# Attention with a low-rank feed-forward layer: one tensor for both q rings, one copy for q's high half, and another order in the DMA queue

## The chip, the cores and the metric

The kernel runs on one core of a Trainium2 chip. The metric is the time of one execution on the device in microseconds. The kernel before takes 2845.18 us, the median of three runs (2844.33 to 2846.65).

## The reference

The input is a batch of 16 sequences of 512 rows with 256 columns. Each row is normalised (layernorm), then goes through causal attention with 32 query heads that share 16 key and value heads in pairs, head width 64, with an ALiBi bias per head, and is added back. The sum is normalised again and goes through a feed-forward layer whose two matrices are products of rank 64, with a gelu between them.

```python
qkv = inputs @ W_qkv                       # 256 -> 2048 (q) + 1024 (k) + 1024 (v)
k, v = repeat(k, 2), repeat(v, 2)          # 16 pairs of query heads
scores = einsum('bhqd,bhkd->bhqk', q, k) / sqrt(64) + slope[h] * (pos_k - pos_q)
scores = where(causal, scores, -inf)
x = x + softmax(scores) @ v @ W_out
P = layernorm(x) @ U1
H = gelu(P @ V1 + b1)
x = x + (H @ U2) @ V2 + b2
```

## The kernel before

Every product is made of fp16 halves: a value is split into a high half and a low half (what is left), and three products (low by high, high by low, high by high) stand for one of fp32. The high half of a projection is made by ScalarE, the low half by VectorE, both out of the PSUM bank into which TensorE projected.

The work is a pipeline over steps. A pass handles one sequence in 16 steps, s = 0 to 15, one step for each key head with its two query heads, and each step has five segments, n = 0 to 4. The first pass fills the pipeline (mode FIRST), 15 passes run full (MID), two more drain it (LAST, TAIL). Within step s these things of different heads lie side by side:

- q of head s is projected (segment 1 of even steps, 2 of odd ones), and in odd steps k of heads s-1 and s together (segment 0).
- `max_scores` (line 509) multiplies q and k of head s-2 for the row maxima, which VectorE takes out of PSUM. After four heads the maxima are transposed (segment 2 of steps 2, 6, 10, 14), split by ScalarE and VectorE (semaphore `lo_m`), and a DMA writes them as two rows (`neg_max_t_hi`, `neg_max_t_lo`) under q, so that the second product of scores already has the maximum taken off. PE waits for these rows at segment 0 of steps 3, 7, 11 and 15.
- `scores` and ScalarE's exponential work on head s-7; ScalarE makes `p_hi`, GpSimd makes `p_lo`.
- `attend` multiplies by v for head s-8, VectorE normalises, ScalarE and GpSimd split the result into the two halves of `o_hi_lo` (GpSimd's half, semaphore `lo_o`, is made in the first segment of the step after), and a transposing DMA brings it into the ring `o_t`. After four heads PE projects them (`project_out`, line 571) and waits for the transposes at segment 4 of steps 12, 0, 4 and 8.
- The feed-forward layer of the sequence before is spread over the remaining places; its result is stored to memory at step 5, and the next sequence's x is loaded at step 1.

q and k are projected two heads to a tile of 128 partitions, but the products of scores want one head with its halves stacked: `q_hi_lo` holds the high half on partitions 0 to 63 and the low half on 64 to 127; `q_hi_aug` holds the high half again, with the ALiBi rows and the maxima's rows below; `k_lo_hi` and `k_hi_aug` are the same for k. So each step copies q by DMA (per step four copies of the high half, two query heads into two rings, and two of the low half), and each odd step k. All these copies, the transposes, the loads and the stores go through one queue, that of SyncE (SP), which issues them in program order: if one waits for a semaphore, all behind it wait. What a step issues, in which order, is written out by hand in `body` of the sync block (from line 379).

TensorE's projections share three PSUM banks. `projection_order` (line 113) lists the uses of a pass in program order, and `PROJ` (line 145) gives use number k the bank k modulo 3; `next_proj` (line 480) makes PE wait until the bank's last user was read. A pass has 76 uses, so the last use of a pass (`out` of step 15, number 75) and the first of the next (`q` of step 0) have the same bank, 0.

Of the kernel before, what the change touches and what calls it, by code (L numbers as in the profile page):

```python
# [23 lines left out]
F16 = mybir.dt.float16  # L24
# [4 lines left out]
P = 128  # L29
D = 256  # L30
DC = D // P
S = 512
# [28 lines left out]
QK_DMAS = 6  # L61
# [50 lines left out]

def projection_order():

    uses = []
    for s in range(KV):
        for n in range(SEG):
            if (s, n) in H_PAIRS:
                uses += [("h", 2 * H_PAIRS[s, n]), ("h", 2 * H_PAIRS[s, n] + 1)]
            if n == MAX_SEG and s % 4 == 2:  # L120
                uses.append(("max", s))
            if (s, n) in X_PAIRS:
                uses.append(("x", X_PAIRS[s, n]))
            if n == K_SEG and s % 2 == 1:
                uses.append(("k", s))
            if n == OUT_SEG:
                uses.append(("out", s))
            if (s, n) in LN2_T_AT:
                uses.append(("ln2", LN2_T_AT[s, n]))
            if n == q_segment(s):  # L130
                uses.append(("q", s))
            if n == V_SEG and s % 8 < 4:
                uses.append(("v", s))
            if (s, n) in U1_AT:
                uses.append(("p", U1_AT[s, n]))
            if (s, n) == Y_AT:
                uses += [("y", 0), ("y", 1)]
            if (s, n) in U2_PAIRS:
                uses.append(("u", U2_PAIRS[s, n]))
    return uses  # L140
# [68 lines left out]
def layer(nc, x, w_qkv, w_out, u1, v1, b1, u2, v2, b2, k_aug, q_aug, ident_d, ident_b_d, causal_d, out):  # L209
    B = x.shape[0]  # L210
    ctx = ExitStack()
    with ctx:
# [23 lines left out]
        qa = sb("q_hi_lo", [P, RING, 2, S], F16)  # L236
        qb = sb("q_hi_aug", [P, RING, 2, S], F16)
# [112 lines left out]
        def _(sp):  # L350
# [28 lines left out]
            def body(i, mode):  # L379
                for s in steps(mode):  # L380
                    g = i * KV + s
                    if s % 4 == 2 and in_stage(mode, s, 6):

                        gr = i * 4 + (s - 6) // 4
                        sp.wait_ge(lo_m, at(gr + 1))
                        r0 = (s - 6) % RING
                        for part in range(2):
                            sp.dma_start(qb[MAX0 + part:MAX0 + part + 1, r0:r0 + 4, :, :].rearrange("o a b (t q) -> o (a b t) q", q=P),
                                         mt[part][:, :]).then_inc(m_in[(s - 6) // 4 % 2], 16)
                    if mode in (FIRST, MID):  # L390
                        if s % 2 == 1:
# [12 lines left out]
                            for j in range(2):  # L404
                                sp.dma_start(ka[0:HD, r0 + j, :], ks[1][j * HD:(j + 1) * HD, :]).then_inc(kdup_in[r0 // 2], 16)
                        r = s % RING
# [4 lines left out]
                        for h in range(2):  # L411
                            mine = qs[0][h * HD:(h + 1) * HD, s % 2, :]
                            sp.dma_start(qb[0:HD, r, h, :], mine).then_inc(qdup_in[r], 16)
                            sp.dma_start(qa[0:HD, r, h, :], mine).then_inc(qdup_in[r], 16)
# [3 lines left out]
                    if in_stage(mode, s, ATT + 1):  # L418
                        slot, kv = s % 2, (s - ATT - 1) % KV
                        sp.wait_ge(lo_o, at(g - ATT))  # L420
                        sp.sem_inc(gate, 1)
                        sp.dma_start_transpose(ot[:, kv % OUT_RING, :, :].rearrange("p a (t q) -> p (a t) q", q=P),  # L422
                                               o_hl[:, slot, :, :].rearrange("p a q -> p (a q)")).then_inc(ot_in[slot], 16)
# [21 lines left out]
        def _(pe):  # L445
# [32 lines left out]
            def body(i, mode):  # L478
# [30 lines left out]
                def max_scores(s, n):  # L509
                    g = i * KV + s - 2  # L510
                    r = (s - 2) % RING
                    if n == 0:
                        use = 2 * i + (s - 2) // RING + 1
                        pe.wait_ge(qdup_in[r], at(QK_DMAS * 16 * use))
                        if s % 2 == 0:
                            pe.wait_ge(kdup_in[r // 2], at(QK_DMAS * 16 * use))
# [158 lines left out]
        def _(act):  # L675
# [29 lines left out]
            def body(i, mode):  # L705
# [24 lines left out]
                def high_k(s):  # L730
                    act.wait_ge(pe_k, at(i * (KV // 2) + (s + 1) // 2))
                    landed = QK_DMAS * 16 * (2 * i + (s - 3) // RING + 1)
# [4 lines left out]
                def high_q(s):  # L737
                    g = i * KV + s
                    act.wait_ge(pe_q, at(g + 1))
                    landed = QK_DMAS * 16 * (2 * i + (s - 2) // RING + 1)  # L740
# [434 lines left out]
```

## Time and profile before

| | |
|---|---|
| time, median of 3 runs | 2845.18 us |
| profiled execution: time, span | 2847.87 us, 2846.1 us |
| PE, ScalarE (ACT), GpSimd (POOL), VectorE (DVE) busy | 94%, 77%, 70%, 70% |
| granted TensorE clock, mean | 0.988 |
| DMA share of 16 engines in q1, the kernel's queue | 42.8% |
| SP queue's wait for GpSimd's `o_hi_lo` | 566.8 us in 235 waits |

PE is the engine that is nearly always busy, and 1.00 of full clock is granted between 79 and 2777 us. What PE waits for there is the question of the profile. A matmul's shown end is modelled: back to back, a 512-column matmul starts 0.22 us after the one before although its row says 0.38, so an idle time that a row shows is about 0.16 us less than the delay.

### The profile page before, as it was taken

The page shows a single profiled execution, that of the slowest core. Times are in us where ns is not written, and L with a number is a line of the kernel's source. Part 1 is how long each engine was busy: PE and PEld are TensorE (multiplying, and loading weights), DVE is VectorE, ACT ScalarE, POOL GpSimd, SP SyncE. Part 2 cuts the span into 40 slices and gives each one's busy share as a digit, 9 for nine tenths or more (in the row PEclk, how much of TensorE's full clock was granted, in tenths as well). Part 3 has the DMA queues.
Part 4 walks back from the last instruction along what each step waited for, and adds up shares of the span by engine and source line. Part 5 has one row for each costly group of instructions (what it writes and reads, how often), then busy time and mean ns, then how long its engine had stood idle before and what let it go on. Part 6 is the DMA issues. An engine that isn't in the chain of part 4 may idle for free.

```text
span 2846.1 us, 83739 instructions
## 1 busy us (share of the span) xinstructions
PE 2688.1 (94%) x31112; PEld 1835.5 (64%) x31112; DVE 1990.9 (70%) x6795; ACT 2178.4 (77%) x3892; POOL 2000.1 (70%) x1816
## 2 busy tenths in 40 slices
PE   4999999999999999999999999999999999999985
PEld 1566666666666666666666666666666666666662
DVE  6667677676766767677676777767667676777743
ACT  3777878778777887878878787787878878787782
POOL 1667777777777777777777777777767777777773
PEclk9999999999999999999999999999999999999996
DMA  6444345344444444444444445434444454445421
GB/s 169 91 97 91 87 99 93 87 96 93 95 88 96 89 91 95 87 99 96 88 95 92 94 88 101 91 87 97 89 95 94 94 87 91 96 88 101 88 45 26
DMA packets 495147, 260.83 MB, mean 92 GB/s; under 512 B 317962, under 2 KB 493066, under 8 KB 494474
## 3 DMA queue, kind: packets, MB, share of 16 engines
q1 hardware_dynamic: 494740, 255.47, 42.8%
q8 instruction: 247, 4.05, 0.6%
q14 instruction: 160, 1.31, 0.1%
HBM read 27.73 MB, written 8.39 MB: 13 GB/s over the span
## 4 chain that ended last, share of the span: by engine, by line
PE 65%; ACT 11%; issue 7%; POOL 5%; DMA 5%; SPq 4%; DVE 3%; ACTq 0%; POOLq 0%; DVEq 0%
PE proj L452 31%; PE scores L452 16%; PE o_acc L452 10%; PE max_scores L452 7%; POOL p_lo L1082 3%; ACT p_hi L677 3%; ACT p_f L718 3%; DMA o_t<-o_hi_lo 2%; ACT L718 2%; DMA q_hi_aug<-neg_max_t_lo 2%; ACT h_f L809 2%; POOL h_lo L1112 1%; POOL o_hi_lo L1094 1%; SPq L422 1%; DVE max_scores L909 1%
## 5 line engine op out<-in xcount | busy, mean ns | idle before, releaser
L1082 POOL TENSOR_TENSOR p_lo<-p_f,p_hi 128x512 f16<-128x512 f32 x1280 | 1481.5, 1169 | 778.7 <-ACT p_hi L677 777.8
L909 DVE CUSTOM_DVE_ANT_0 max_scores<-max_scores,causal 128x512 f32<-128x512 f32 (+3 forms) x2048 | 970.0, 507 | 313.7 <-PE max_scores L452 299.6
L718 ACT ACTIVATE p_f<-scores 128x512 f32<-128x512 f32 x1280 | 755.7, 590 | 169.0 <-PE scores L452 143.2
L677 ACT ACTIVATE p_hi<-p_f 128x512 f16<-128x512 f32 x1280 | 800.0, 625 | 14.2
L452 PE MATMUL scores<-q_hi_lo,k_lo_hi 128*128 128x512 f16 (+3 forms) x2048 | 614.4, 300 | 34.5 <-ACT p_f L718 18.3
L452 PE MATMUL scores<-q_hi_aug,k_hi_aug 128*128 128x512 f16 (+3 forms) x2048 | 586.1, 299 | 0.0
L452 PE MATMUL o_acc<-v_hi_one,p_lo 128*128 128x65 f16 x5120 | 517.2, 194 | 8.8 <-POOL p_lo L1082 7.8
L452 PE MATMUL max_scores<-k_hi_aug,q_hi_aug 96*128 96x512 f16 (+3 forms) x2048 | 489.8, 300 | 29.0 <-issue 17.5
L452 PE MATMUL o_acc<-v_hi_one,p_hi 128*128 128x65 f16 x5120 | 517.0, 194 | 0.0
L452 PE MATMUL o_acc<-v_lo,p_hi 128*128 128x64 f16 x5120 | 516.4, 193 | 0.0
L452 PEld LDWEIGHTS o_acc<-v_hi_one,p_lo 128*128 128x128 f16 x5120 | 471.2, 98 | 41.5 <-POOL p_lo L1082 22.8
L452 PEld LDWEIGHTS o_acc<-v_lo,p_hi 128*128 128x128 f16 x5120 | 468.1, 98 | 38.5
L452 PEld LDWEIGHTS o_acc<-v_hi_one,p_hi 128*128 128x128 f16 x5120 | 467.4, 97 | 0.0
L452 PE MATMUL scores<-ident_bf,causal 128*128 128x128 bf16 x2048 | 448.1, 219 | 0.0
L452 PE MATMUL proj<-wo_hi,o_t 128*128 128x256 f16 x2048 | 382.2, 275 | 13.7 <-DMA o_t<-o_hi_lo 13.6
L452 PE MATMUL proj<-xn_t_hi,wqkv_lo 128*128 128x512 f16 x768 | 293.6, 382 | 28.8 <-DVE x_acc L916 16.4
L1094 POOL TENSOR_TENSOR o_hi_lo<-o_f,o_hi_lo 128x512 f16<-128x512 f32 x256 | 296.3, 1157 | 3.4 <-ACT o_hi_lo L677 3.4
L452 PE MATMUL proj<-xn_t_hi,wqkv_hi 128*128 128x512 f16 x768 | 293.1, 382 | 0.0
L452 PE MATMUL proj<-xn_t_lo,wqkv_hi 128*128 128x512 f16 x768 | 293.0, 381 | 0.0
L909 DVE DVE_READ_ACCUMULATOR2_ANT row_max<- 128x1 f32 x2048 | 284.2, 139 | 1.3
L452 PE MATMUL proj<-wo_lo,o_t 128*128 128x256 f16 x1024 | 280.8, 274 | 0.0
L452 PEld LDWEIGHTS scores<-q_hi_lo,k_lo_hi 128*128 128x128 f16 x2048 | 199.6, 97 | 114.3 <-ACT p_f L718 24.8
(107 smaller groups left out, 4282.4 us busy)
## 6 DMA issues: line engine op xcount, KB each, us to landing
q_hi_aug<-q_pair_hi SPq DMA_DIRECT2D x512, 64.0 KB, 2.0
q_hi_lo<-q_pair_hi SPq DMA_DIRECT2D x512, 64.0 KB, 2.0
q_hi_lo<-q_pair_lo SPq DMA_DIRECT2D x512, 64.0 KB, 2.0
k_hi_aug<-k_pair_hi SPq DMA_DIRECT2D x256, 64.0 KB, 2.0
k_lo_hi<-k_pair_hi SPq DMA_DIRECT2D x256, 64.0 KB, 2.0
k_lo_hi<-k_pair_lo SPq DMA_DIRECT2D x256, 64.0 KB, 2.0
x_rows<-in_L_attn_inputs SPq DMA_DIRECT2D x17, 512.0 KB, 4.5
x_acc<-in_L_attn_inputs SPq DMA_DIRECT2D x64, 128.0 KB, 2.5
```

Source lines behind the costliest of these rows:

```text
L422: sp.dma_start_transpose(ot[:, kv % OUT_RING, :, :].rearrange("p a (t q) -> p (a t) q", q=P), o_hl[:, slot, :, :].rearrange("p a q -> p (a ...
L452: return nc.tensor.matmul(out_ap, lhs, rhs, start=start, stop=stop, skip_group_check=True)
L677: return nc.scalar.activation(out_ap, in_ap, ACT.Copy, scale=scale)
L718: nc.scalar.activation(p_f[:, k % 3, :], score_bank[k % 2][:, :], ACT.Exp).then_inc(exp_done, 1)
L809: nc.scalar.activation(h_f[:, c % 2, :], proj("h", c)[:, :], ACT.Gelu_apprx_tanh, bias=b1c[:, c:c + 1], scale=1.0 / FFN_SCALE).then_inc(ge ...
L909: last = nc.vector.tensor_tensor_reduce(out=bank, in0=bank, in1=causal[:, (T - 1 - qt) * P:S], scale=1.0, scalar=-3e38, op0=ALU.add, op1=A ...
L1082: nc.gpsimd.tensor_tensor(p_lo[:, slot, n, :], p_f[:, k % 3, :], p_hi[:, slot, n, :], ALU.subtract).then_inc(lo_p, 1)
L1094: nc.gpsimd.tensor_tensor(o_hl[:, slot, 1, :], o_f[:, slot, :, :].rearrange("p t c -> p (t c)"), o_hl[:, slot, 0, :], ALU.subtract).then_i ...
L1112: nc.gpsimd.tensor_tensor(h_lo[:, c % 2, :], h_f[:, c % 2, :], h_hi[:, c % 2, :], ALU.subtract).then_inc(lo_h, 1)
```

## The change

1. The two q rings become one tensor `q_operands` with an index in front; `qa` and `qb` are its two halves. The high half of a head is copied to both by one DMA whose source is read twice. Per step q takes 4 DMAs on the SP queue in place of 6 (`Q_DMAS` 4; `K_DMAS` stays 6).
2. The transposing DMA of a head is no longer the last thing of its step, but stands in the step after: behind k's copies in odd steps, at the start in even steps, in each case ahead of the maxima's rows and of q. It is the same wait (`lo_o`) for the same head. What was behind it in its old step (the loads of x and of the residual, the store) is now ahead of it.
3. `SKIP_BANK` adds an unused entry to the order of projection uses behind q of steps 6 and 7. A pass has 78 uses, and all uses from the maxima of step 6 on have another bank than before.

```diff
-QK_DMAS = 6
+K_DMAS, Q_DMAS = 6, 4
...
+SKIP_BANK = (6, 7)
...
             if n == q_segment(s):
                 uses.append(("q", s))
+                if s in SKIP_BANK:
+                    uses.append(("skip", s))
...
-        qa = sb("q_hi_lo", [P, RING, 2, S], F16)
-        qb = sb("q_hi_aug", [P, RING, 2, S], F16)
+        qab = sb("q_operands", [P, 2, RING, 2, S], F16)
+        qa, qb = qab[:, 0, :, :, :], qab[:, 1, :, :, :]
...
             def body(i, mode):
                 for s in steps(mode):
                     g = i * KV + s
-                    if s % 4 == 2 and in_stage(mode, s, 6):
-
-                        gr = i * 4 + (s - 6) // 4
-                        sp.wait_ge(lo_m, at(gr + 1))
-                        r0 = (s - 6) % RING
-                        for part in range(2):
-                            sp.dma_start(qb[MAX0 + part:MAX0 + part + 1, r0:r0 + 4, :, :].rearrange("o a b (t q) -> o (a b t) q", q=P),
-                                         mt[part][:, :]).then_inc(m_in[(s - 6) // 4 % 2], 16)
                     if mode in (FIRST, MID):
                         if s % 2 == 1:
                             r0 = (s - 1) % RING
...
                             sp.wait_ge(lo_k, at(i * (KV // 2) + (s + 1) // 2))
                             for j in range(2):
                                 sp.dma_start(ka[0:HD, r0 + j, :], ks[1][j * HD:(j + 1) * HD, :]).then_inc(kdup_in[r0 // 2], 16)
+                    if in_stage(mode, s, ATT + 2):
+                        slot, kv = (s - 1) % 2, (s - ATT - 2) % KV
+                        sp.wait_ge(lo_o, at(g - ATT - 1))
+                        sp.sem_inc(gate, 1)
+                        sp.dma_start_transpose(ot[:, kv % OUT_RING, :, :].rearrange("p a (t q) -> p (a t) q", q=P),
+                                               o_hl[:, slot, :, :].rearrange("p a q -> p (a q)")).then_inc(ot_in[slot], 16)
+                    if s % 4 == 2 and in_stage(mode, s, 6):
+
+                        gr = i * 4 + (s - 6) // 4
+                        sp.wait_ge(lo_m, at(gr + 1))
+                        r0 = (s - 6) % RING
+                        for part in range(2):
+                            sp.dma_start(qb[MAX0 + part:MAX0 + part + 1, r0:r0 + 4, :, :].rearrange("o a b (t q) -> o (a b t) q", q=P),
+                                         mt[part][:, :]).then_inc(m_in[(s - 6) // 4 % 2], 16)
+                    if mode in (FIRST, MID):
                         r = s % RING
                         if s % 2 == 0 and SEG * (i * KV + s - 7) > 0:
                             sp.wait_ge(pe_scores, at(SEG * (i * KV + s - 7)))
...
                         sp.wait_ge(hi_q, at(g + 1))
                         for h in range(2):
                             mine = qs[0][h * HD:(h + 1) * HD, s % 2, :]
-                            sp.dma_start(qb[0:HD, r, h, :], mine).then_inc(qdup_in[r], 16)
-                            sp.dma_start(qa[0:HD, r, h, :], mine).then_inc(qdup_in[r], 16)
+                            sp.dma_start(qab[0:HD, :, r, h, :], mine.unsqueeze(1).to_broadcast([HD, 2, S])).then_inc(qdup_in[r], 16)
                         sp.wait_ge(lo_q, at(g + 1))
                         for h in range(2):
                             sp.dma_start(qa[HD:P, r, h, :], qs[1][h * HD:(h + 1) * HD, s % 2, :]).then_inc(qdup_in[r], 16)
-                    if in_stage(mode, s, ATT + 1):
-                        slot, kv = s % 2, (s - ATT - 1) % KV
-                        sp.wait_ge(lo_o, at(g - ATT))
-                        sp.sem_inc(gate, 1)
-                        sp.dma_start_transpose(ot[:, kv % OUT_RING, :, :].rearrange("p a (t q) -> p (a t) q", q=P),
-                                               o_hl[:, slot, :, :].rearrange("p a q -> p (a q)")).then_inc(ot_in[slot], 16)
                     if s in range(OUT_LAG - 2, OUT_LAG + 2) and mode in (FIRST, MID):
                         t = s - (OUT_LAG - 2)
...
                     r = (s - 2) % RING
                     if n == 0:
                         use = 2 * i + (s - 2) // RING + 1
-                        pe.wait_ge(qdup_in[r], at(QK_DMAS * 16 * use))
+                        pe.wait_ge(qdup_in[r], at(Q_DMAS * 16 * use))
                         if s % 2 == 0:
-                            pe.wait_ge(kdup_in[r // 2], at(QK_DMAS * 16 * use))
+                            pe.wait_ge(kdup_in[r // 2], at(K_DMAS * 16 * use))
                             pe.wait_ge(kaug_in[r // 2], at(16 * use))
                     bank, back = max_place(s, n)
                     if SEG * g + n + 1 - back > 0:
```

PE's and ScalarE's waits on the copies likewise count 4 for q and 6 for k.

The queue of SP in a full pass, around an odd step. Before, the transpose that ended step 6 stands ahead of the k copies of step 7:

```order
L422 DMA_TRANSPOSE o_t<-o_hi_lo 128x8x128 [waits lo_o]
L396 DMA k_hi_aug<-in_k_aug 10x1024 [waits pe_scores]
L401 DMA k_hi_aug<-k_pair_hi 64x512 [waits hi_k]
L402 DMA k_lo_hi<-k_pair_hi 64x512
L401 DMA k_hi_aug<-k_pair_hi 64x512
L402 DMA k_lo_hi<-k_pair_hi 64x512
L405 DMA k_lo_hi<-k_pair_lo 64x512 [waits lo_k]
L405 DMA k_lo_hi<-k_pair_lo 64x512
L413 DMA q_hi_aug<-q_pair_hi 64x512 [waits hi_q]
```

After, it stands behind them. `q_operands` is the one tensor for the two rings.

```order
L393 DMA k_hi_aug<-in_k_aug 10x1024 [waits pe_scores]
L398 DMA k_hi_aug<-k_pair_hi 64x512 [waits hi_k]
L399 DMA k_lo_hi<-k_pair_hi 64x512
L398 DMA k_hi_aug<-k_pair_hi 64x512
L399 DMA k_lo_hi<-k_pair_hi 64x512
L402 DMA k_lo_hi<-k_pair_lo 64x512 [waits lo_k]
L402 DMA k_lo_hi<-k_pair_lo 64x512
L407 DMA_TRANSPOSE o_t<-o_hi_lo 128x8x128 [waits lo_o]
L425 DMA q_operands<-q_pair_hi 64x2x512 [waits hi_q]
```

What moved: the k copies are ahead of the wait for `lo_o`, and the copy of q's high half writes both rings.

The queue of SP at the end of step 5 and the start of step 6 of a full pass, before (`out` is the store of a finished sequence, `neg_max_t` are the maxima's rows):

```order
L417 DMA q_hi_lo<-q_pair_lo 64x512 [waits lo_q]
L417 DMA q_hi_lo<-q_pair_lo 64x512
L422 DMA_TRANSPOSE o_t<-o_hi_lo 128x8x128 [waits lo_o]
L437 DMA out<-x_rows 128x4x256 [waits y_done]
L388 DMA q_hi_aug<-neg_max_t_hi 1x32x128 [waits lo_m]
L388 DMA q_hi_aug<-neg_max_t_lo 1x32x128
L413 DMA q_hi_aug<-q_pair_hi 64x512 [waits pe_scores,hi_q]
L414 DMA q_hi_lo<-q_pair_hi 64x512
```

And now:

```order
L428 DMA q_operands<-q_pair_lo 64x512 [waits lo_q]
L428 DMA q_operands<-q_pair_lo 64x512
L442 DMA out<-x_rows 128x4x256 [waits y_done]
L407 DMA_TRANSPOSE o_t<-o_hi_lo 128x8x128 [waits lo_o]
L415 DMA q_operands<-neg_max_t_hi 1x32x128 [waits lo_m]
L415 DMA q_operands<-neg_max_t_lo 1x32x128
L425 DMA q_operands<-q_pair_hi 64x2x512 [waits pe_scores,hi_q]
L425 DMA q_operands<-q_pair_hi 64x2x512
```

What moved: the store of 512 KB is issued behind q's copies and ahead of the transpose's wait, no longer between the transpose and the maxima's rows.

PE at segment 1 of step 0, from one sequence to the next, before:

```order
L452 MATMUL scores<-q_hi_aug,k_hi_aug 128x512
L452 MATMUL max_scores<-k_hi_aug,q_hi_aug 128x384 [waits max_done]
L452 MATMUL max_scores<-k_hi_aug,q_hi_aug 128x128
L452 MATMUL proj<-xn_t_hi,wqkv_lo 128x512 [waits acc_done,lo_ln1]
L452 MATMUL proj<-xn_t_lo,wqkv_hi 128x512
```

After:

```order
L457 MATMUL scores<-q_operands,k_hi_aug 128x512
L457 MATMUL max_scores<-k_hi_aug,q_operands 128x384 [waits max_done]
L457 MATMUL max_scores<-k_hi_aug,q_operands 128x128
L457 MATMUL proj<-xn_t_hi,wqkv_lo 128x512 [waits lo_ln1]
L457 MATMUL proj<-xn_t_lo,wqkv_hi 128x512
```

No matmul moved. The projection of q waits only for the normalised input's low half (`lo_ln1`), no longer for the addition (`acc_done`) that reads the output projection of step 15. The output projection of step 6 in turn has the bank of q of step 6, and waits for that q's low half (`lo_q`) in place of an addition of step 5.

## Rows read from the trace of the kernel before

**Rows 1.** Windows: us, busy PE, PEld, DVE, ACT, POOL; clock; DMA; GB/s.

```profile
79.00:2777.00 2698.00, 2615.65 (x30769) 1802.54 (x30770) 1915.21 (x6621) 2141.57 (x3843) 1970.02 (x1787) 1.00 0.44 91
```

**Rows 2.** Waits of PE, 170 to 2720 us: total, times, longest.

```profile
PE proj L452 <- DVE x_acc L916: 16.4, 14, 1.2
PE scores L452 <- DMA q_hi_aug<-neg_max_t_lo: 14.5, 16, 1.5
PE max_scores L452 <- issue: 11.4, 14, 1.6
PE proj L452 <- DMA o_t<-o_hi_lo: 7.5, 12, 1.1
```

**Rows 3.** Timeline, step 0 of a full pass: start, length, engine, tiles [idle before].

```profile
1522.49 0.69 DVE L836 SCALAR_TENSOR_TENSOR xn_t_lo<-proj,xn_t_hi 128x512 f16<-128x512 f32 x1 [0.46 <-ACT xn_t_hi L677]
1523.10 0.42 DVE L916 SCALAR_TENSOR_TENSOR x_acc<-proj,x_acc 128x256 f32<-128x256 f32 x1
...
1523.66 0.38 PE L452 MATMUL proj<-xn_t_hi,wqkv_lo 128*128 128x512 f16 x1 [1.18 <-DVE x_acc L916]
```

**Rows 4.** Timeline, step 7 to the start of step 8, of several engines.

```profile
1597.64 0.60 ACT L677 ACTIVATE k_pair_hi<-proj 128x512 f16<-128x512 f32 x1 [0.49 <-PE proj L452]
...
1597.86 1.16 POOL L1094 TENSOR_TENSOR o_hi_lo<-o_f,o_hi_lo 128x512 f16<-128x512 f32 x1
...
1600.98 0.47 SPq L401 DMA_DIRECT2D k_hi_aug<-k_pair_hi  x1
...
1603.41 1.23 SPq L405 DMA_DIRECT2D k_lo_hi<-k_pair_lo  x2
...
1606.97 0.38 PE L452 MATMUL max_scores<-k_hi_aug,q_hi_aug 96*128 96x512 f16 x1 [1.41 <-issue]
```

**Rows 5.** Tiles k_lo_hi, neg_max_t_lo, o_hi_lo, in this order: DMA issue to landing.

```profile
DMA to landing us min/median/max: 1.9/2.0/3.9
...
DMA to landing us min/median/max: 1.9/2.5/4.9
...
DMA to landing us min/median/max: 3.0/3.1/5.1
```

**Rows 6.** Timeline, steps 5 to 7 of another pass.

```profile
2098.17 1.23 SPq L417 DMA_DIRECT2D q_hi_lo<-q_pair_lo  x2
...
2103.00 0.58 SPq L437 DMA_DIRECT2D out<-x_rows  x1
...
2104.72 0.60 SPq L388 DMA_DIRECT2D q_hi_aug<-neg_max_t_lo  x1
...
2108.51 0.39 PE L452 MATMUL scores<-q_hi_lo,k_lo_hi 128*128 128x512 f16 x1 [1.43 <-DMA q_hi_aug<-neg_max_t_lo]
```

**Rows 7.** Page, DMA issues: count, KB each, median us to landing.

```profile
x_rows<-in_L_attn_inputs SPq DMA_DIRECT2D x17, 512.0 KB, 4.5
x_acc<-in_L_attn_inputs SPq DMA_DIRECT2D x64, 128.0 KB, 2.5
out<-x_rows SPq DMA_DIRECT2D x16, 512.0 KB, 3.3
```

**Rows 8.** Timeline of SP's queue in steps 1 and 2.

```profile
2054.45 1.24 SPq L417 DMA_DIRECT2D q_hi_lo<-q_pair_lo  x2
...
2059.41 0.58 SPq L433 DMA_DIRECT2D x_rows<-in_L_attn_inputs  x1
```

**Rows 9.** Timeline: step 8 around `out`; step 6, q's low half and `out`.

```profile
1606.54 1.16 POOL L1094 TENSOR_TENSOR o_hi_lo<-o_f,o_hi_lo 128x512 f16<-128x512 f32 x1
...
1613.32 0.27 PE L452 MATMUL proj<-wo_hi,o_t 128*128 128x256 f16 x1
...
1593.27 0.67 DVE L836 SCALAR_TENSOR_TENSOR q_pair_lo<-proj,q_pair_hi 128x512 f16<-128x512 f32 x1
...
1594.08 0.10 PEld L452 LDWEIGHTS proj<-wo_hi,o_t 128*128 128x128 f16 x1
```

**Rows 10.** Waits of PE, the filling pass, 60 to 150 us.

```profile
PE max_scores L452 <- issue: 6.1, 4, 2.9
```

More of the change, by code:

```diff
@@ L731, in high_k @@
                     act.wait_ge(pe_k, at(i * (KV // 2) + (s + 1) // 2))
-                    landed = QK_DMAS * 16 * (2 * i + (s - 3) // RING + 1)
+                    landed = K_DMAS * 16 * (2 * i + (s - 3) // RING + 1)
                     if landed > 0:
@@ L739, in high_q @@
                     act.wait_ge(pe_q, at(g + 1))
-                    landed = QK_DMAS * 16 * (2 * i + (s - 2) // RING + 1)
+                    landed = Q_DMAS * 16 * (2 * i + (s - 2) // RING + 1)
                     if landed > 0:
```

## The prediction

> **What bounds the kernel.** I read the windows first. In the 2698 us between fill and drain PE is busy for 2615.65 us and its clock is granted in full [rows 1]. No other engine comes near; so the time there is PE's stream of matmuls plus the gaps in it, and a change that removes no matmul can win only gaps. Next I read PE's waits over the full passes. The four that the change can touch add up to 49.8 us: 16.4 on the addition `x_acc`, 14.5 on the maxima's rows, 11.4 at `max_scores` with no releaser named, 7.5 on the transposes [rows 2]. Then the timeline at each of these places, because a wait that goes is worth only what lies between it and the next thing that is late. Fifteen passes run full, so 1 us per pass is 15 us, 0.5% of the time. The shown idle time of each wait is 0.16 us short of the delay, as the table's note says.
>
> **The bank of q at step 0 (`SKIP_BANK`).** PE's projection of q starts at 1523.66, 0.14 us after `x_acc` ended at 1523.52 [rows 3]. It is that wait which goes: after the change the bank's last user is a tile that was read long before. But the same matmul also waits for the normalised input's low half, which VectorE ends at 1523.18 [rows 3], directly before `x_acc`. So it can start at 1523.18 + 0.14 = 1523.32, which is 0.34 us earlier and not the whole 1.35. There are 14 such waits [rows 2]: 14 x 0.34 = 4.8 us. The bounds are 0 (VectorE does not report sooner) and 14 x 1.34 = 18.8 us (if q waited only for the bank). I take 4.8, since both waits stand on the same instruction in the program. The row that will then be named is `xn_t_lo`.
>
> **k's copies ahead of the transpose.** In step 7 ScalarE has k's high half ready at 1597.64 + 0.60 = 1598.24, but the first copy is issued at 1600.98. The queue stood at the transpose, whose source GpSimd finished at 1597.86 + 1.16 = 1599.02; after that came the transpose's own issue (1.3 us) and the ALiBi rows. The low copies go out from 1603.41, the second at about 1604.05, and PE starts `max_scores` of step 8 at 1606.97, with 1.41 us idle [rows 4]. The profile names no releaser, yet a copy takes 2.0 us to land and up to 3.9 [rows 5], and the last of six is the last thing this matmul lacks. Without the wait it would start at 1606.97 - 1.41 - 0.16 = 1605.40. After the change the first copy is issued at 1598.3, the last 3.1 us later (1604.05 - 1600.98), at 1601.4, and lands at 1603.4, in the worst case of the rows at 1605.3: in time either way. Eleven of the 14 waits without a name stand at step 8 and hold 10.0 of the 11.4 us [rows 2]: 10.0 + 11 x 0.16 = 11.8 us. The other three, 1.4 us, stand at step 14; there passes that do not wait lose 0.34 us a little later at `attend`, so most comes back: 0.5 us. In the filling pass the same wait holds 6.1 us, of which the first, 2.9, comes before any transpose and stays [rows 10]; of the rest I take 3.0. Together 15.3 us; bounds 0 (if the wait is something else) and 11.8 + 1.9 + 3.7 = 17.4. The transposes of odd steps go out about 3 us later. Their heads are the first or third of a group of four, while PE waits for the fourth, whose transpose is in an even step and is not moved against its neighbours.
>
> **The store and the loads ahead of the transpose.** The last of the maxima's two rows is issued at 2104.72, and PE takes up scores at 2108.51 after 1.43 us idle; unhindered it would have been 2108.51 - 1.43 - 0.16 = 2106.92 [rows 6]. The row lands in 1.9 us at best, in 2.5 at the median [rows 5]; at best that is 2106.62, early by 0.30 us. Why is it late? The 512 KB store is issued at 2103.00 [rows 6], takes 3.3 us [rows 7], and so lies on the same DMA engines. It sits there only because it stood behind the transpose. Now it stands behind q's copies, the last of which ended their issue at 2098.17 + 1.23 = 2099.40 [rows 6], and four issues of 0.6 us have become two. It goes out by 2099.4 and is gone by 2102.7, before the maxima's rows. The load of x at step 1 moves alike: from 2059.41 to behind 2054.45 + 1.24 = 2055.69 [rows 8], landing 4.5 us later [rows 7], at 2060.2, when it now would land at 2063.9. Of the 16 waits [rows 2] ten are at step 7, four at step 3 (behind the load of x), two at step 15 (behind a residual load of 128 KB, which moves ahead too). Worth: 14.5 + 16 x 0.16 = 17.1 us, if all go. They will not all go at step 7: with a margin of 0.30 us a landing at the median of 2.5 would still be late by 2.5 - 1.9 - 0.30 = 0.3 us, times 15 = 4.5; at the best landing nothing is left. I keep 4.0 and count 13.1 us. Bounds: 0 and 17.1.
>
> **One copy for q's high half.** 256 steps issue two copies fewer of 0.60 us: 307 us of SP's queue, none of it on PE's path by itself. The wait for GpSimd swallows it at most places (566.8 us of waiting in the table), and what it does for k and for the store is counted above. The merged copy moves 128 KB. No row shows its landing; the nearest are 2.0 us (64 KB, the same kind) [rows 5] and 2.5 us (128 KB from memory) [rows 7], the outer bound 4.5 us for 512 KB. I take 2.3. q of step s is first used in step s+2, some 10 us after its copy, so even 4.5 costs nothing. The Trainium skill ("DMA: Bandwidth & Descriptors", Anatomy of one DMA) fits a copy at about 2.0 us plus its bytes over 436 GB/s, which gives 2.3 us for 128 KB; an estimate by that page that leaves the sum as it is.
>
> **The transposes.** 7.5 us in 12 waits [rows 2], half of them at step 8. There GpSimd ends at 1606.54 + 1.16 = 1607.70, so the transpose can land at 1607.7 + 0.1 + 3.1 = 1610.9 [rows 5, 9]. PE reaches `out` at 1613.32 [rows 9], after the change 1.57 us sooner, at 1611.75: 0.85 us to spare. Now the queue issues some of these about 1 us late; that goes, but PE also comes sooner. I count 0, with bounds of +9 (landings up to 5.1 us make it late more often) and -9.4 (all waits gone: 7.5 + 12 x 0.16).
>
> **Sum.** 4.8 + 15.3 + 13.1 + 0 = 33.2 us. Against the profiled execution (2847.9 us, 1.8 of them outside its span) that is 2814.7; this execution stood 2.7 us above the median of the runs, and on the median it is 2845.2 - 33.2 = 2812.0.
>
> **Rivals.**
> - *The maxima's rows stay late.* The transpose that stands directly ahead of them is issued about 2.4 us before and needs 3.1 to land [rows 5]; if it, not the store, holds them up, its place is unchanged and 13.1 us stay: 2825.1. For: single waits at steps without a store. Against: ten of 16 stand behind the store and all the others behind a load.
> - *What step 8 gains is given back at step 8's `out`.* The margin of 0.85 us holds at 3.1 us, not from 3.95 on. If the landings there are mostly longer, the 11.8 us return as waits on `o_t`: 2823.8.
> - *No change.* The Trainium skill ("DMA: Bandwidth & Descriptors", Issuing engines are not separate DMA queues) says that what the issuing sequencer spends on a DMA is usually small beside the DMA itself, which speaks against gaining by the queue's order and number of issues. Here an issue of 0.60 us stands against a landing of 2.0, but the queue is one line of some ten issues per step plus a wait for GpSimd. As a mechanism of this kernel: the merged copy costs 1.2 us to issue and the last k copy lands no sooner, since its two low copies wait for VectorE; then 15.3 and 13.1 stay and only the bank's 4.8 is left: 2840.4, or with a little loss 2843.
> - *Slower: the transposes land late everywhere.* The four steps per pass at which PE waits for a fourth transpose are 60 in all. If the 128 KB copies in flight push its landing from 3.1 to 4.9 us, each costs 4.9 - 3.1 - 0.85 = 1.0 us: 60 us lost against 33 won, 2872. It decides from 0.55 us per wait, a landing of 4.5. Against: q's copies are issued well before the even transposes, and the bytes are the same.
> - A small one: `out` of step 6 now has q's bank. The low half of q ends at 1593.27 + 0.67 = 1593.94, the weights load at 1594.08 [rows 9]: a margin of 0.14 us. If VectorE slips by 0.3 us, it costs 15 x 0.16 = 2.4 us. It is inside the range.
>
> **How the numbers follow.** Forecast 0.62 (2812, own range 2802 to 2819); maxima's rows 0.14 (2825); given back 0.08 (2824); no change 0.08 (2840 to 2845, half of it under the limit); slower 0.05 (2872); the rest, 0.03, lies below 2802 with the transposes' waits gone too. A measurement of this kernel tells 0.2%, 5.7 us, from no change. Faster: 0.62 + 0.14 + 0.08 + 0.03 + 0.04 = 0.91; same 0.04; slower 0.05. The range from 2800 to 2828 takes in the first three cases and leaves out 16 in 100.
>
> **What would show it.** Right: PE's wait on `x_acc` is replaced by one of about 0.85 us on `xn_t_lo`; no unnamed wait of `max_scores` at step 8; the wait on `neg_max_t_lo` at most 5 us in sum and none at step 3; SP issues k's first copy within 0.1 us of ScalarE's end in step 7; wait on `o_t` still 5 to 12 us. Wrong: a wait on `neg_max_t_lo` of over 10 us, one on `o_t` of over 15 us, or a new one on `q_pair_lo` at step 6.

## The result and the profile after

The changed kernel takes 2811.4 us, the median of four runs (2809.6 to 2813.7), against 2845.9 us for the kernel before in the same comparison (2844.3 to 2848.5). The ratio is 0.9878, 95% interval 0.9861 to 0.9895: about 34.5 us or 1.2% less. The forecast was 2812. The same program timed again on another occasion gave 2809.5 us and 0.9871 (0.9857 to 0.9885).

Between fill and drain, as in [rows 1]: the window, then us, busy PE, PEld, DVE, ACT, POOL, clock, DMA share, GB/s.

```profile
78.00:2742.00 2664.00, 2610.65 (x30783) 1803.51 (x30783) 1915.81 (x6623) 2137.69 (x3847) 1971.98 (x1790) 1.00 0.46 93
```

PE is busy for nearly as long as before (2610.65 against 2615.65 us) at the same full clock; the stretch is 34 us shorter. No matmul went: the 5 us are, by my estimate, the 0.16 us at each wait by which a matmul's shown end is too late and which counts as busy; some thirty waits fewer make 4.8 us. So the time came out of the gaps. PE's waits of the full passes, which answer to [rows 2] (total, times, longest):

```profile
PE scores L457 <- ACT p_f L723: 13.2, 42, 0.3
PE proj L457 <- DVE xn_t_lo L841: 10.5, 14, 0.8
PE proj L457 <- DMA o_t<-o_hi_lo: 6.7, 11, 1.2
PE o_acc L457 <- POOL p_lo L1087: 4.5, 16, 1.8
PE scores L457 <- DVE row_max L914: 1.5, 2, 0.8
PE scores L457 <- DMA q_operands<-neg_max_t_lo: 1.5, 3, 1.0
```

The wait on `x_acc` (16.4) is one on `xn_t_lo` (10.5), the unnamed one of `max_scores` (11.4) is gone from the full passes, the one on the maxima's rows fell from 14.5 to 1.5, and the one on the transposes stayed (7.5 to 6.7). Then I looked at each place in the timeline. Step 0, against [rows 3]:

```profile
1500.79 0.69 DVE L841 SCALAR_TENSOR_TENSOR xn_t_lo<-proj,xn_t_hi 128x512 f16<-128x512 f32 x1 [0.46 <-ACT xn_t_hi L682]
...
1501.40 0.41 DVE L921 SCALAR_TENSOR_TENSOR x_acc<-proj,x_acc 128x256 f32<-128x256 f32 x1
...
1501.54 0.39 PE L457 MATMUL proj<-xn_t_hi,wqkv_lo 128*128 128x512 f16 x1 [0.76 <-DVE xn_t_lo L841]
```

PE now starts while `x_acc` is still being added, 0.06 us after `xn_t_lo` ended (1501.48) where I had put 0.14. Steps 7 and 8 of the same pass as [rows 4]:

```profile
1575.53 0.60 ACT L682 ACTIVATE k_pair_hi<-proj 128x512 f16<-128x512 f32 x1 [0.49 <-PE proj L457]
...
1575.74 1.16 POOL L1099 TENSOR_TENSOR o_hi_lo<-o_f,o_hi_lo 128x512 f16<-128x512 f32 x1
...
1576.15 0.46 SPq L398 DMA_DIRECT2D k_hi_aug<-k_pair_hi  x1
...
1578.57 1.23 SPq L402 DMA_DIRECT2D k_lo_hi<-k_pair_lo  x2
...
1579.92 1.28 SPq L407 DMA_TRANSPOSE o_t<-o_hi_lo  x1
...
1583.27 0.38 PE L457 MATMUL max_scores<-k_hi_aug,q_operands 96*128 96x512 f16 x1
```

ScalarE has k's high half at 1576.13, and the first copy goes out 0.02 us later; before it was 2.74 us. GpSimd ends at 1576.90, which no longer matters to k. `max_scores` of step 8 has no idle time. The store and the maxima's rows in steps 5 to 7, against [rows 6]:

```profile
2069.55 1.25 SPq L428 DMA_DIRECT2D q_operands<-q_pair_lo  x2
2070.85 0.59 SPq L442 DMA_DIRECT2D out<-x_rows  x1
2073.18 1.26 SPq L407 DMA_TRANSPOSE o_t<-o_hi_lo  x1
2075.58 0.58 SPq L415 DMA_DIRECT2D q_operands<-neg_max_t_hi  x1
2076.21 1.72 SPq L415 DMA_DIRECT2D q_operands<-neg_max_t_lo  x1
```

The store goes out 5.4 us ahead of the maxima's low row (2070.85 and 2076.21), where it was 1.7 us ahead of it. Issue to landing of `neg_max_t_lo`, `q_pair_hi` (the merged copy) and `o_hi_lo`, us min/median/max, against [rows 5]:

```profile
DMA to landing us min/median/max: 1.9/1.9/3.5
...
DMA to landing us min/median/max: 2.4/2.5/4.5
...
DMA to landing us min/median/max: 3.0/3.1/5.0
```

The median of the maxima's low row fell from 2.5 to 1.9 us. By the step in which the row is issued, the medians were 3.6 us at step 2 (behind the load of x), 2.5 at step 6 (behind the store), 2.1 at step 10 and 1.9 at step 14; now all four are 1.9. So it was the 512 KB in flight that made the rows late, and it was at the two steps that have one.

The merged copy lands in 2.5 us, not in the 2.3 that I took. The formula of the Trainium skill ("DMA: Bandwidth & Descriptors", Anatomy of one DMA) also gives 2.3, but the page fitted it to DMAs that GpSimd issues, and these go out on SP's queue.

### The profile page after: what moved, and what is told of

The parts are those of the page before. It is cut to its first block, busy times and chain, and to the rows that moved or that the text cites. A ratio compares the mean times of both kernels' runs of the same rounds, so it can differ in the third digit from the quotient of the medians.

```text
span 2810.1 us, 83227 instructions
## 1 busy us (share of the span) xinstructions
PE 2685.6 (96%) x31112; PEld 1837.4 (65%) x31112; DVE 1990.8 (71%) x6795; ACT 2171.9 (77%) x3892; POOL 1999.6 (71%) x1816
## 4 chain that ended last, share of the span: by engine, by line
PE 71%; ACT 10%; issue 6%; POOL 6%; DMA 3%; DVE 3%; SPq 0%; ACTq 0%; POOLq 0%; DVEq 0%
PE proj L457 34%; PE scores L457 18%; PE o_acc L457 12%; PE max_scores L457 7%; POOL p_lo L1087 4%; ACT p_f L723 3%; ACT p_hi L682 2%; DMA o_t<-o_hi_lo 2%; ACT L723 2%; ACT h_f L814 2%; POOL h_lo L1117 2%; DMA o_t<-in_L_attn_W_out 1%; DVE xn_t_lo L841 1%; DMA q_operands<-neg_max_t_lo 1%; PE proj L593 1%
## 5 line engine op out<-in xcount | busy, mean ns | idle before, releaser
L457 PE MATMUL scores<-q_operands,k_lo_hi 128*128 128x512 f16 (+3 forms) x2048 | 614.3, 300 | 22.7 <-ACT p_f L723 17.7
L457 PE MATMUL scores<-q_operands,k_hi_aug 128*128 128x512 f16 (+3 forms) x2048 | 586.4, 299 | 0.0
L457 PE MATMUL max_scores<-k_hi_aug,q_operands 96*128 96x512 f16 (+3 forms) x2048 | 490.7, 301 | 14.0 <-DVE row_max L914 9.1
L457 PEld LDWEIGHTS scores<-ident_bf,causal 128*128 128x128 bf16 x2048 | 200.2, 98 | 100.9 <-issue 0.2
```

Of the source, the lines that this page charges most:

```text
L457: return nc.tensor.matmul(out_ap, lhs, rhs, start=start, stop=stop, skip_group_check=True)
```

## The experiments

The runs form a table of the change's three parts, alone and together. Beside the ratio of the times stands a second measure from one profiled execution each: from PE's first `scores` of step 0 of the second full pass to that of step 7 of the fifteenth, 13.4 passes (in the changed kernel from 321.7 to 2584.1 us). It leaves out the start and the end, which differ by some us between executions. Two executions of the changed kernel differ by 2.8 us in it; a difference of that size says nothing.

| kernel | time, median us | ratio (95%) | 13.4 passes, us |
|---|---|---|---|
| before | 2846 to 2849 | 1 | 2291.6 |
| bank alone | 2843.6 | 0.9979 (0.9970 to 0.9988) | 2287.7 |
| merged copy alone | 2844.5 | 0.9995 (0.9987 to 1.0004) | 2286.7 |
| order alone | 2822.5 | 0.9910 (0.9895 to 0.9925) | 2270.9 |
| order and merged copy | 2818.9 | 0.9896 (0.9883 to 0.9910) | 2268.2 |
| order and bank | 2820.0 | 0.9899 (0.9885 to 0.9912) | 2268.6 |
| all three, the changed kernel | 2811.4 / 2809.5 | 0.9878 / 0.9871 | 2262.4 / 2259.6 |

**The changed kernel without the skipped bank** (order and merged copy).

```diff
-SKIP_BANK = (6, 7)
+SKIP_BANK = ()
```

> The changed kernel with no skipped bank entries; all else as changed. My theory (the bank's wait covers a second one that ends 0.34 us sooner, 0.42 us in the changed kernel's trace): PE waits for x_acc again at step 0, about 1.2 us shown in each of 14 passes in place of 0.76 on xn_t_lo, and the time is 14 x 0.42 = 5.9 us more: 2817. Rival (the bank was the only thing in the way): 14 x 1.35 = 19 us more, 2830. Third: nothing, 2811.

2818.9 us, 5 to 7 us above the two timings of the changed kernel by the ratios. PE's wait:

```profile
PE proj L457 <- DVE x_acc L921: 16.3, 14, 1.2
```

The rival is out: the addition is late with the new queue too, and the skipped bank is what removes the wait. For the time, the intervals of the ratios overlap; the 13.4 passes (2268.2 against 2262.4 and 2259.6 us) tell the two kernels apart.

**Two copies for q's high half** (order and bank).

```diff
-K_DMAS, Q_DMAS = 6, 4
+K_DMAS, Q_DMAS = 6, 6
...
-                            sp.dma_start(qab[0:HD, :, r, h, :], mine.unsqueeze(1).to_broadcast([HD, 2, S])).then_inc(qdup_in[r], 16)
+                            sp.dma_start(qb[0:HD, r, h, :], mine).then_inc(qdup_in[r], 16)
+                            sp.dma_start(qa[0:HD, r, h, :], mine).then_inc(qdup_in[r], 16)
```

> The changed kernel with q's high half again copied by two DMAs of 64 KB in place of one of 128 KB; order and banks as changed. My theory (each gap goes with the order of the queue, the number of issues is hidden by the queue's waiting): 2811 to 2815, no wait on k's copies at step 8. Rival (the queue was too full, and the 307 us of issue time saved are what lets k and the maxima through): most of the 34 us come back, 2835 or more, with waits of max_scores at step 8.

2820.0 us: 6 to 8 us lost by the ratios, and 6.2 to 9.0 in the 13.4 passes. My expectation missed. The waits, then the queue before step 8's `out`:

```profile
PE proj L458 <- DMA o_t<-o_hi_lo: 10.3, 16, 1.3
...
PE scores L458 <- DMA q_operands<-neg_max_t_lo: 2.9, 7, 0.6
```

```profile
918.20 1.78 SPq L425 DMA_DIRECT2D q_operands<-q_pair_hi  x1
...
919.39 1.16 POOL L1100 TENSOR_TENSOR o_hi_lo<-o_f,o_hi_lo 128x512 f16<-128x512 f32 x1
...
920.02 0.60 SPq L426 DMA_DIRECT2D q_operands<-q_pair_hi  x1
...
920.66 1.23 SPq L429 DMA_DIRECT2D q_operands<-q_pair_lo  x2
...
922.01 1.24 SPq L407 DMA_TRANSPOSE o_t<-o_hi_lo  x1
...
926.09 0.27 PE L458 MATMUL proj<-wo_hi,o_t 128*128 128x256 f16 x1 [1.33 <-DMA o_t<-o_hi_lo]
```

GpSimd's half is ready at 920.55, the queue is still issuing q's copies, and the transpose goes out 1.46 us late; PE pays 1.33. In the changed kernel's same pass GpSimd ends at 914.81, and:

```profile
911.83 2.07 SPq L428 DMA_DIRECT2D q_operands<-q_pair_lo  x2
...
913.65 1.16 POOL L1099 TENSOR_TENSOR o_hi_lo<-o_f,o_hi_lo 128x512 f16<-128x512 f32 x1
...
914.90 1.25 SPq L407 DMA_TRANSPOSE o_t<-o_hi_lo  x1
```

The queue waits for GpSimd again. Counted over the 15 transposes that step 8 needs, 9 are issued over 0.2 us late with two copies (mean delay 0.50 us) and none with the merged one (0.09).

**The loads and the store behind the transpose again.**

```diff
                         sp.dma_start_transpose(ot[:, kv % OUT_RING, :, :].rearrange("p a (t q) -> p (a t) q", q=P),
                                                o_hl[:, slot, :, :].rearrange("p a q -> p (a q)")).then_inc(ot_in[slot], 16)
+                    if s - 1 in range(OUT_LAG - 2, OUT_LAG + 2) and mode in (FIRST, MID):
+                        t = s - 1 - (OUT_LAG - 2)
...
+                    if s - 1 == X_LOAD and mode in (FIRST, MID):
...
+                    if s == (STORE_AT if mode == TAIL else STORE_AT + 1) and ffn_in(i, s):
...
-                    if s in range(OUT_LAG - 2, OUT_LAG + 2) and mode in (FIRST, MID):
-                        t = s - (OUT_LAG - 2)
...
-                    if s == X_LOAD and mode in (FIRST, MID):
...
-                    if s == STORE_AT and ffn_in(i, s):
```

> The changed kernel with the loads of x and of the residual and the store issued directly behind the transpose in the step after, as they were before the change; k's copies stay ahead of the transpose. My theory (the 512 KB ahead of the maxima's rows delays them): PE's wait on neg_max_t_lo is back at 12 to 15 us over the full passes at steps 7, 3 and 15, and the time is 13 us more: 2824; no waits of max_scores at step 8. Rival (the transpose directly ahead of the rows is what delays them, and the gain there came from a shorter queue): 2811.

2826.9 us, 0.9926 (0.9912 to 0.9939): 14 to 16 us lost, with k's copies still ahead of the transpose. The maxima's low row again lands late at just the two steps with 512 KB ahead of it: medians of 3.9 us at step 2 and 2.4 at step 6, against 2.0 and 1.9 at steps 10 and 14.

```profile
PE scores L457 <- DMA q_operands<-neg_max_t_lo: 14.6, 18, 1.6
```

**The transpose ahead of k's copies again.**

```diff
+                    if in_stage(mode, s, ATT + 2):
+                        slot, kv = (s - 1) % 2, (s - ATT - 2) % KV
...
                     if mode in (FIRST, MID):
                         if s % 2 == 1:
                             r0 = (s - 1) % RING
...
-                    if in_stage(mode, s, ATT + 2):
-                        slot, kv = (s - 1) % 2, (s - ATT - 2) % KV
...
```

> The changed kernel with the transpose ahead of k's copies in odd steps too; loads and store ahead of it, one copy for q's high half, banks as changed. My theory (k's copies stood behind the transpose's wait): max_scores waits again at step 8, 10 us shown in some 11 passes and 2 to 3 us in the filling pass, and the time is 15 us more: 2826. Rival (fewer issues let k through even so): 2811 to 2815.

2833.7 us, 0.9947 (0.9934 to 0.9959): 20 to 22 us lost where 15 were expected.

```profile
PE max_scores L457 <- issue: 17.8, 15, 1.5
```

Fourteen of these 15 waits stand at step 8 and hold 17.3 us, more and longer than in the kernel before (11 waits, 10.0 us). The trace of the kernel before shows why. In the 10 full passes in which PE waited for the maxima's rows at step 7, its wait at step 8 was 0.42 us in the mean, and the four passes without any wait at step 8 are all among them; in the other 5 it was 1.16 us. A wait at step 7 gives k's copies time, so it hides part of the wait at step 8; with the rows in time, PE meets all of it. Put back singly, the parts cost, against 0.9878, 5 + 6 + 14 + 20 = 45 us, while together they bring 34.5: k's place in the queue is worth more once the rows are in time.

**The changed kernel once more** (program unaltered), and **with 128 more semaphore instructions on PE at its start**, which shift where in its program PE stands at a given time.

```diff
+            for _ in range(128):
+                pe.sem_inc(gate, 1)
             pe.sem_inc(pe_pp, FREE)
```

> The changed kernel once more, so that the others of this group have it beside them on the same chip. 0.9878 of the kernel before, as measured.

> The changed kernel with 128 instructions more on PE at its very start, where PE waits for its first input in any case; they only count up a semaphore that nobody waits for. 
2809.5 and 2812.2 us (0.9882, 0.9868 to 0.9897). The waits on `o_t` at step 8 were in passes 2, 4, 13, 15 and again 4, 11, 13, 15; with the shift they are in 1, 3, 12, 14. So the passes that are hit moved with PE's instruction count, in the one shift that was tried; what this is comes at the end.

**The merged copy alone**, on the kernel before.

```diff
-QK_DMAS = 6
+K_DMAS, Q_DMAS = 6, 4
...
-        qa = sb("q_hi_lo", [P, RING, 2, S], F16)
-        qb = sb("q_hi_aug", [P, RING, 2, S], F16)
+        qab = sb("q_operands", [P, 2, RING, 2, S], F16)
+        qa, qb = qab[:, 0, :, :, :], qab[:, 1, :, :, :]
...
-                            sp.dma_start(qb[0:HD, r, h, :], mine).then_inc(qdup_in[r], 16)
-                            sp.dma_start(qa[0:HD, r, h, :], mine).then_inc(qdup_in[r], 16)
+                            sp.dma_start(qab[0:HD, :, r, h, :], mine.unsqueeze(1).to_broadcast([HD, 2, S])).then_inc(qdup_in[r], 16)
```

> The kernel before with q's high half written to both rings by one DMA and nothing else changed: order of the queue and banks as before. Putting two copies back cost 6 us, not the 0 to 3 I had expected; the theory that follows from that trace (the shorter queue lets the transpose of step 7 out in time, so that step 8 waits less on it, and the filling pass gains a little): 3 to 6 us faster than before, 2840 where before is 2845; the wait on o_t falls from 7.5 to about 4, that of max_scores at step 8 stays at 10 or grows. Rival (merging does nothing by itself): no change.

2844.5 us, 0.9995 (0.9987 to 1.0004): no change that can be told, and the expected 3 to 6 us missed. One trace of each shows less waiting in the full passes: the waits on the transposes fall from 7.5 to 4.0, as expected, and the 13.4 passes are 4.9 us shorter. From step 7 of the filling pass to step 7 of the next it took 156.5 us in place of 154.3.

**The bank alone and the order alone**, on the kernel before. The first adds only the skipped entry:

```diff
+SKIP_BANK = (6, 7)
...
                 uses.append(("q", s))
+                if s in SKIP_BANK:
+                    uses.append(("skip", s))
```

The second is the changed kernel with both other parts undone, as in the first two experiments:

```diff
-SKIP_BANK = (6, 7)
+SKIP_BANK = ()
...
-K_DMAS, Q_DMAS = 6, 4
+K_DMAS, Q_DMAS = 6, 6
```

> The kernel before with the unused entry in the order of projection uses alone. Theory (what goes is the wait on x_acc, and PE then waits for xn_t_lo directly before it, worth 0.42 us in each of 14 passes by the changed kernel's trace): 6 us faster, a ratio of 0.998; PE's wait on x_acc is gone and one of about 10.5 us on xn_t_lo stands in its place; the waits on the maxima's rows (14.5) and without a name (11.4) stay. Rival (what PE gains at step 0 is given back at step 3 or 8, where it is then earlier at a thing that is late anyway): within 2 us of no change, 1.000.

> The kernel before with the new order of the DMA queue alone: q's high half still goes out in two copies, and the order of projection uses has no unused entry. Theory A (the three parts act one by one, the order carries most): the run without the skipped bank lost 5 us against the changed kernel, the one with two copies 6 us, so this one loses 11 of 34: 23 us faster than before, a ratio of 0.992, with PE's wait on x_acc back at about 16 us in 14 waits. Theory B (the gains overlap, so the copy and the bank are worth less without one another): 27 to 30 us faster, 0.990.

The bank alone brings 6.0 us by the ratio, as expected:

```profile
PE scores L457 <- DMA q_hi_aug<-neg_max_t_lo: 12.4, 18, 1.4
PE max_scores L457 <- issue: 12.2, 18, 1.6
PE proj L457 <- DVE xn_t_lo L841: 10.5, 14, 0.8
```

In the 13.4 passes it is 3.9 us; the rival that PE gives some of it back later is not excluded, since the wait without a name (12.2 against 11.4) and that on `o_t` (9.2 against 7.5) are a little longer.

The order alone brings 0.9910, 25.6 us, between the theories. The three alone sum to 33.0 us by the ratios, 29.5 in the 13.4 passes, against 34.7 to 36.7 and 29.2 to 32.0 for all three. Within these measurements the bank, the merged copy and the order add up. What does not is the order's own two halves: undone last they cost 14 and 20 us, while the whole order alone brings 25.6.

**What is left at step 0, and the maxima's rows ahead of the transpose.** The changed kernel's wait on `xn_t_lo` comes from ScalarE, which makes the high half of o first (1499.65) and then that of x:

```profile
1499.65 0.63 ACT L682 ACTIVATE o_hi_lo<-o_f 128x512 f16<-128x512 f32 x1 [0.36 <-DVE o_f L933]
...
1500.18 0.58 ACT L682 ACTIVATE xn_t_hi<-proj 128x512 f16<-128x512 f32 x1
```

One move puts the x block ahead of the o block at segment 4 of step 15; another puts the maxima's rows ahead of the transpose in SP's queue. Both moves, then each alone:

```diff
+                        if (s, n) in X_PAIRS and mode in (FIRST, MID):
...
+                            high_x(i + 1, X_PAIRS[s, n])
                         if n == O_SEG and in_stage(mode, s, ATT + 1):
...
-                        if (s, n) in X_PAIRS and mode in (FIRST, MID):
...
-                            high_x(i + 1, X_PAIRS[s, n])
...
+                    if s % 4 == 2 and in_stage(mode, s, 6):
...
                     if in_stage(mode, s, ATT + 2):
...
-                    if s % 4 == 2 and in_stage(mode, s, 6):
```

> The changed kernel with two orders more: on ScalarE the normalised input's second high half is made ahead of the high half of o in step 15, and on SP the maxima's rows go ahead of the transpose in steps 2, 6, 10 and 14. My theory (q of step 0 waits for xn_t_lo, and that for ScalarE, which idles 0.36 us for o_f just before it; xn_t_lo can then start when VectorE comes free, 0.46 us sooner, and attend follows at 0.42 us sooner): 14 x 0.42 = 5.9 us less than the changed kernel, and up to 2 us less from the maxima's rows. Rival (GpSimd's p_lo holds attend up right behind q, so that PE waits there instead): 0 to 1 us less, with a new wait of o_acc on p_lo at step 0 in each pass.

> The changed kernel with one move on ScalarE: at segment 4 of step 15 the high half of the normalised input is made ahead of the high half of o. Theory (the wait on xn_t_lo at step 0, 10.5 us in 14, is what ScalarE's order leaves): 4 to 6 us less than the changed kernel, a ratio of 0.9855, the wait on xn_t_lo about 2 us. Rival (the gain of the kernel with both moves came from the maxima's rows): as the changed kernel, 0.9875.

> The changed kernel with one move on SP's queue: the maxima's rows are issued ahead of the transpose. Theory (late rows come from packets of instruction loading, not from the transpose ahead of them; issuing 1.3 us sooner covers part): 0 to 2 us less than the changed kernel, 0.9865 to 0.9875; the wait on the maxima's rows about 1.4 us or less. Rival (the transpose ahead of the rows is what makes them late): no wait on them at all and 3 us or more less.

Both: 2803.8 us, 0.9851 (0.9836 to 0.9866). The x block alone: 2805.3 us, 0.9850 (0.9837 to 0.9864). The rows alone: 2812.1 us, 0.9872 (0.9858 to 0.9885). The gain is ScalarE's order, 6 to 8 us beyond the changed kernel. The intervals overlap slightly, but the 13.4 passes (2254.8 and 2256.4 us, against 2259.6 and 2262.4) and the wait agree. The maxima's rows waited 2.1 us in 6 waits when issued first, where 1.4 or less was expected. With the x block first, the wait, then step 0:

```profile
PE proj L457 <- DVE xn_t_lo L841: 2.1, 14, 0.2
```

```profile
1493.93 0.63 ACT L682 ACTIVATE xn_t_hi<-proj 128x512 f16<-128x512 f32 x1
...
1494.43 0.64 ACT L682 ACTIVATE o_hi_lo<-o_f 128x512 f16<-128x512 f32 x1
...
1494.98 0.69 DVE L841 SCALAR_TENSOR_TENSOR xn_t_lo<-proj,xn_t_hi 128x512 f16<-128x512 f32 x1
...
1495.72 0.39 PE L457 MATMUL proj<-xn_t_hi,wqkv_lo 128*128 128x512 f16 x1 [0.15 <-DVE xn_t_lo L841]
```

## Why the prediction was right, point by point

**What bounds it, and the sum.** Right: no matmul went, PE's busy time moved by 5 us of 2616, and 36.0 us of span went against 33.2 forecast. 29.2 of them fall in the 13.4 passes, 5.9 before and 0.9 behind.

**The bank, forecast 4.8 us.** Segment 1 of step 0 shortened by 0.42 us per pass, 5.9 in 14; the bank alone gave 6.0 (3.4 to 8.5). The mechanism holds (the row is `xn_t_lo`, 0.75 us a pass where 0.85 was forecast), and the size was a little short: PE started 0.06 us after VectorE's end and not 0.14.

**k's copies, forecast 15.3 us.** The full-pass part (11.8) came whole: no unnamed wait is left there. Undone last, this order costs 20 us; no run has it alone, so what it brings to the kernel before by itself is open. In the filling pass the three later unnamed waits (3.2 us shown) went, and one of 1.1 us came at another step; from step 7 to its end the pass is 1.8 us shorter, where I had counted 3.0. At step 14 the return that I had counted is seen: `attend` waits 0.18 us for `p_lo` in 15 of 15 passes.

**The store and loads, forecast 13.1 us.** 14 to 16 us when undone. The mechanism holds. By the starts of the matmuls 4.2 us of delay stay of 18.2, and 3.7 of them stand at step 7, against 4.0 forecast; step 3 is clear. That this remainder came out is luck. I had let every pass be 0.3 us late, with a landing that keeps its median of 2.5 us. But that median was itself the work of the store and the load; it is now 1.9, ten of the 15 passes lose under 0.1 us at step 7, and three single late landings make 3.0 of the 3.7 us. The rival that the transpose ahead of the rows makes them late is out: issuing them ahead of it brought nothing (0.9872 against 0.9871 and 0.9878).

**The merged copy, forecast 0: the term that was mis-sized.** With the rest of the change it is worth 6 to 8 us by the ratios; alone it shows 4.9 us in the full passes of one trace, and nothing clear in the time. I had written that the wait for GpSimd swallows the two saved issues at most places, and that q's copies are issued well before the even transposes. The second is what failed: at step 8 the transpose was issued over 0.2 us behind GpSimd in 10 of 15 passes of the kernel before (mean 0.83 us), and q's copies are what the queue was busy with. The new order alone leaves 11 of 15 late (mean 0.49), the merged copy none. My section on the transposes had this ("about 1 us late; that goes") and gave it no price of its own, because PE was to come sooner as well. Both happened, so the two nearly cancel in the sum: 6.7 us in 11 waits against 7.5 in 12. That makes the transposes' 0 right as a net value and the copy's 0 wrong as a part's value. The page named in the "no change" rival (the Trainium skill, "DMA: Bandwidth & Descriptors", Issuing engines are not separate DMA queues) calls the sequencer's time per DMA usually small beside the DMA. Here 1.2 us of it per step stood ahead of the one transfer that PE waits for, and it showed in the time.

**The other rivals.** "No change" and "slower" are out; the transposes land at the same median, 3.1 us, beside the 128 KB copies. "Given back at step 8" is out in the net, but with two copies it happened in part: 5.9 of the 10.3 us on `o_t` stand there. The small one (`q_pair_lo` at step 6) did not occur.

## What to carry to other kernels

A queue that issues in program order is an engine of its own: ask at each semaphore wait in it what stands behind it, which engine lacks that, and how many issues stand between the last producer and the transfer that ends a wait. Fewer issues pay only where the queue arrives after its producer, so count the places at which it does, not its waiting in total. Where two waits follow each other on the bounding engine, removing the first exposes the second, and undoing parts one at a time then adds up to more than the whole.

## What the runs showed of the hardware that was not expected

DMAs of one size land at the median of 1.9 us or as late as 3.5, and the late landings go with packets of two queues that the profile calls `instruction`, on the same 16 DMA engines. The changed kernel's page lists them (packets, MB, share):

```profile
q8 instruction: 247, 4.05, 0.6%
q14 instruction: 156, 1.28, 0.1%
```

The 247 packets of queue 8 are one per 11 us, of 16 KB each. The DMA view of two stretches, each from the issue of a maxima's low row until 3.6 us later: first one that landed after 3.5 us, then one that landed after 1.9.

```profile
q1 hardware_dynamic: 495, 0.22, 29.6%
q8 instruction: 1, 0.02, 2.4%
q14 instruction: 1, 0.01, 1.0%
...
q_operands<-neg_max_t_lo SPq DMA_DIRECT2D x1, 8.0 KB, 3.5
```

```profile
q1 hardware_dynamic: 417, 0.31, 41.0%
...
q_operands<-neg_max_t_lo SPq DMA_DIRECT2D x1, 8.0 KB, 1.9
```

Counted over the changed kernel's 64 rows, from issue to landing: of the 20 that landed after more than 2.3 us all overlap a packet of queue 8, of the 44 others 4 do, each for at most 0.2 us at one end. For the transposes, late being over 3.6 us, it is 68 of 72 late ones and 48 of 184 others. The 4 late ones that are left met a packet of queue 14, and of the 113 transposes that met neither queue none was late. In the run with 128 more instructions on PE it is 20 of 21 and 4 of 43 for the rows, while the passes that are hit moved. Of the 14 waits on `o_t` and on the maxima's rows that remain in the full passes, 13 were ended by a DMA that met a packet of queue 8; a margin of 1.6 us for the rows (3.5 - 1.9) and 1.9 for the transposes (5.0 - 3.1) would cover them. That the late landing is tied to these packets is shown by the counts and, by one run, by the shift. How one 16 KB packet holds up a transfer spread over 16 engines was not measured, and about a quarter of the transposes that landed in time met one too.
